# Cross-attention: GpSimd instead of SyncE issues the four transfers a pair that restack K's low part

## The reference

```
x = x + xattn(layernorm(x), ctx)     # 16 heads of 16, softmax over 256 keys, no mask and no scale
x = x + attn(layernorm(x))           # 16 heads of 64, causal
x = x + ffn(layernorm(x))            # 256 -> 1024 -> 256, gelu, fake-quantized weights and activations

xattn:  q = queries @ Wq;  k = keys @ Wk;  v = values @ Wv
        out = softmax(q k^T) v, heads joined, @ Wo
```

## Time and profile before

| | |
|---|---|
| runs | 670.81, 672.53 and 673.95 us; median 672.53 us |
| profiled execution | span 669.4 us from its first to its last instruction (the profile gives no other time of it) |
| PE busy | 608.3 us (91%) |
| DVE, ACT, POOL busy | 469.9, 388.8 and 197.3 us |
| PE clock granted | 0.987 of full on average |
| DMA | 58.44 MB, of which q1 moved 36.85, q0 12.20 and q10 8.78 |

### The profile page before, as it was taken

One profiled execution on the slowest core, in us unless ns is written; L12 is line 12 of the kernel. 1 busy time (PEld: TensorE's weight loads), 2 busy tenths in 40 slices (PEclk: granted clock), 3 DMA queues, 4 the chain that ended last, 5 costly groups with the idle time before them and its releaser, 6 DMA issues. The chain is left out here.

```text
span 669.4 us, 18523 instructions
## 1 busy us (share of the span) xinstructions
PE 608.3 (91%) x6772; PEld 520.5 (78%) x6796; DVE 469.9 (70%) x989; ACT 388.8 (58%) x1017; POOL 197.3 (29%) x308
## 2 busy tenths in 40 slices
PE   6788799999999899979998999999999999788997
PEld 3577788888989788865887898888888897644597
DVE  4376867878787677875789847575756656467797
ACT  3386767888888687874351515242424333357895
POOL 4736234545454544400020303030312111250000
PEclk9899989999999899999999999999999999899999
DMA  7888958585857586720300000000000000000012
GB/s 252 184 236 215 269 143 208 139 211 139 210 136 186 117 199 146 171 52 3 125 2 1 2 1 0 0 0 0 0 0 0 2 1 2 9 3 0 1 43 84
DMA packets 35597, 58.44 MB, mean 87 GB/s; under 512 B 6912, under 2 KB 15232, under 8 KB 35552
## 3 DMA queue, kind: packets, MB, share of 16 engines
q1 hardware_dynamic: 25008, 36.85, 21.8%
q0 software_dynamic: 5952, 12.20, 7.5%
q10 hardware_dynamic: 4592, 8.78, 4.8%
HBM read 17.96 MB, written 2.10 MB: 30 GB/s over the span
## 5 line engine op out<-in xcount | busy, mean ns | idle before, releaser
L573 ACT ACTIVATE Pr<-pS,nmax 128x256 f32<-128x256 f32 x256 | 119.8, 480 | 25.1 <-DVE nmax L677 24.5
L677 DVE TENSOR_REDUCE nmax<-pS 128x2 f32<-128x512 f32 x128 | 87.4, 683 | 35.6 <-PE pS L416 35.2
L899 POOL TENSOR_TENSOR a_Pr<-a_Pr,a_rinv 128x512 f32<-128x512 f32 x32 | 32.8, 1045 | 185.8 <-DVE a_rinv L1188 185.8
L426 PE MATMUL pT<-ident,Pr 128*128 128x128 f32 x512 | 78.5, 276 | 0.1
L416 PE MATMUL pS<-Kst,Qst 96*128 96x256 f32 x256 | 57.2, 305 | 21.6 <-DMA Kst<-KSl 16.6
L341 POOL TENSOR_TENSOR CSl<-CT,CSh 128x1024 fp32r<-128x1024 f32 x15 | 35.3, 2355 | 114.5 <-ACT CSh L566 114.5
L271 POOL DMA_DIRECT2D Qst<-QSh x124 | 62.0, 503 | 13.7 <-DVE QSl L649 6.9
L416 PEld LDWEIGHTS pS<-Kst,Qst 96*128 96x128 f32 x256 | 41.5, 192 | 30.2 <-issue 15.2
L1068 ACT ACTIVATE a_Pr<-a_Pr 128x512 f32<-128x512 f32 x32 | 20.2, 631 | 76.0 <-DVE a_Pr L1180 76.0
L426 PEld LDWEIGHTS pT<-ident,Pr 128*128 128x128 f32 x512 | 60.1, 142 | 0.8 <-ACT Pr L573 0.4
L573 ACT ACTIVATION_READ_ACCUMULATOR Pr<-pS,nmax 128x1 f32 x256 | 54.1, 211 | 0.0
(11 more groups left out here) (269 smaller groups left out, 1925.1 us busy)
## 6 DMA issues: line engine op xcount, KB each, us to landing
Kst<-KSh SPq DMA_DIRECT2D x126, 128.0 KB, 2.9
CT<-ctxT ACTq DMA_DIRECT2D x16, 512.0 KB, 5.6
Kst<-KSl SPq DMA_DIRECT2D x63, 128.0 KB, 3.7
Qst<-QSh POOLq DMA_DIRECT2D x124, 64.0 KB, 2.1
Qst<-QSl POOLq DMA_DIRECT2D x62, 64.0 KB, 2.1
X<-x SPq DMA_DIRECT2D x4, 512.0 KB, 9.0
out<-X SPq DMA_DIRECT2D x8, 256.0 KB, 2.2
raw<-awq SPq DMA_DIRECT2D x1, 1024.0 KB, 5.9
```

The source lines that it names most:

```text
L426: last = pe.transpose(pT[s % 2][:, t, k, :], Pr[s % 2][:, t, P * k:P * k + P], ident[:, :])
L573: act.activation(Pr[c % 2][:, t, :], pS[c % 2][:, t, :], ACT.Exp, bias=nmax[c % 2][:, t:t + 1], accum_out=rsum[par][:, c // 4, 2 * (c % 4) ...
L677: dve.tensor_reduce(nmax[s % 2][:, :], pS[s % 2][:, :, :], AX.X, ALU.max, negate=True).then_inc(maxed, 1)
L899: pool.tensor_tensor(rows, rows, rinv[s][:, :].unsqueeze(2).to_broadcast([P, 8, SQ]), ALU.mult).then_inc(weighted, 1)
```

## The change

SP now issues only the eight transfers of K's high part for the pairs 2 to 15 (`pieces=(0, 1)`). POOL issues the four of the low part (`pieces=(2,)`) behind its Q transfers of the same parity, after waits on the same two semaphores. The low part counts on semaphores of its own, `kst_low`, so PE, ACT and DVE wait for both counts. The prologue (pairs 0 and 1) keeps all twelve on SP and ACT, on `kst_in`.

```diff
     RESTACK = 12 * 16
+    LOW = 4 * 16
...
+        def k_restacked(eng, b, n):
+
+            eng.wait_ge(kst_in[b], RESTACK + (n - 1) * (RESTACK - LOW))
+            after(eng, kst_low[b], (n - 1) * LOW)
+
-        def restack_k(eng, b, r, chunks_done, groups=range(4)):
+        def restack_k(eng, b, r, chunks_done, groups=range(4), pieces=(0, 1, 2), done=None):
             after(eng, lo, r + 1)
             apart(eng, waited)
             after(eng, scores, chunks_done)
+            apart(eng, waited)
             for jj in groups:
-                for u, part in enumerate((HI, HI, LO)):
+                for u in pieces:
+                    part = (HI, HI, LO)[u]
                     eng.dma_start(f32(Kst[b][32 * u:32 * u + 32, jj:HP:4, :]),
-                                  f32(KS[part][32 * jj:32 * jj + 32, :, :])).then_inc(kst_in[b], 16)
+                                  f32(KS[part][32 * jj:32 * jj + 32, :, :])
+                                  ).then_inc((done or kst_in)[b], 16)
...
-                    restack_k(sp, 0, EV0 + EV * i + 5, CHUNKS * (p + 1))
+                    restack_k(sp, 0, EV0 + EV * i + 5, CHUNKS * (p + 1), pieces=(0, 1))
...
-                    restack_k(sp, 1, EV0 + EV * i + 9, CHUNKS * (p + 2))
+                    restack_k(sp, 1, EV0 + EV * i + 9, CHUNKS * (p + 2), pieces=(0, 1))
...
                     restack_q(pool, qst_in[0], 0, EV0 + EV * i + 3, CHUNKS * (2 * i + 1))
+                    restack_k(pool, 0, EV0 + EV * i + 5, CHUNKS * (2 * i + 1), pieces=(2,), done=kst_low)
                     ctx_low(1, 2 * i + 4)
                     restack_q(pool, qst_in[1], 1, EV0 + EV * i + 3, CHUNKS * (2 * i + 2))
+                    restack_k(pool, 1, EV0 + EV * i + 9, CHUNKS * (2 * i + 2), pieces=(2,), done=kst_low)
...
-                    pe.wait_ge(kst_in[par], RESTACK * (i + 1 + s // 16))
+                    k_restacked(pe, par, i + 1 + s // 16)
...
-                eng.wait_ge(kst_in[(ahead - 1) % 2], RESTACK * (i + (ahead + 1) // 2))
+                k_restacked(eng, (ahead - 1) % 2, i + (ahead + 1) // 2)
```

More of the change, by code:

```diff
@@ L219, in cross_attention @@
         kst_in = [sem(f"kst_in{i}") for i in range(2)]
+        kst_low = [sem(f"kst_low{i}") for i in range(2)]
         qst_sync, qst_in = sem("qst_sync"), [sem(f"qst_in{i}") for i in range(2)]
```

## The result

| | before | change |
|---|---|---|
| median of the runs | 672.23 us (20 runs) | 668.13 us (20 runs) |
| ratio | | 0.9948, 95% interval 0.9929 to 0.9966 |
| span of the profiled execution | 669.4 us | 666.3 us |

A forecast was written before the change was run, and what follows sets the result against it. PE, busy 91% and in order, was taken as the bound: its work plus its waits, chiefly for K. Terms 1.7 + 2.6 + 2.7 + 4.2 = 11.2 us off 672.5 gave 661.3 us, range 654 to 670.

The forecast's parts named there:

- POOL's price and cover: POOL's low-part issues: 0.7 us each (bounds 0.5 and 1.0), costing nothing, covered by POOL's 4.6 us idle stretch before CSl.
- Pair 11, 4.2 us: Pair 11's K: POOL's stop moves to pair 8, the wait falls from 2.96 to about 0.4, the clock holds: 4.2 us.
- Pairs 4 and 15, 1.7 us: PE's waits for K of 0.42 and 1.29 us both go, as SP is done 2.7 us sooner: 1.7 us gained.
- Pairs 5, 7, 9 and 13, 2.7 us: Odd pairs' K: two queues fill the engines better, 0.7 us a pair, giving back 2.7 of 3.62 us of waits.
- the reading of "0.88 busy" as SP's pace: Even pairs' K: with DMA engines 0.88 busy at 206 GB/s, SP's issuing was taken as the limit.
- the one with the engines as the bound: Rival: odd pairs' K and pair 3's land as before; gain 6.8 us, 665.7, or 3.3 us, 669.2; chance 0.20.
- the one in which the wait is only renamed: Rival: PE waits for K's high part instead, or ACT and DVE hold it up; 672.5 us; chance 0.10.
- Pairs 2 and 3, 2.6 us: Pair 2's wait of 1.61 us goes and pair 3's falls by 1.0 to 3.8: 2.6 us (bounds 1.6 and 8.9).
- The added waits, nothing: PE, ACT and DVE wait for a second count fourteen times; costed at nothing unless the low part is later.
- Short waits at their full length, windows of 32.42 us: Even pair to even pair: a wait costs its full length, so windows without pair 7's or 9's wait are 32.42 us.

The follow-up runs named there:

- e1: The kernel before, K still all on SP, with 13 small POOL transfers added in the prologue to move POOL's stop: 668.8 us, ratio 0.9926.
- e13: The change with PE waiting for K last, its high part after the low part: 667.5 us, ratio 0.9936.
- e14: e10 with PE waiting for K last: 666.3 us, ratio 0.9894 to the kernel before.
- e2: The change without POOL's transfers of K's low part from pair 2 on: 661.1 us, ratio 0.9792 to the kernel before.
- e3: The change with POOL issuing the low part in the order of head groups 2, 3, 0, 1: 665.1 us, ratio 0.9877 to the kernel before.
- e8: The change run again unaltered, with a second profile: 667.9 us, ratio 0.9912 to the kernel before.
- e9: e1 with three weight loads of quad 0 moved to the last quad, behind pair 15's K: 662.7 us, ratio 0.9847 to the kernel before.
- e17: e12 with PE waiting for K last, all of K on SP: 660.3 us, ratio 0.9830 to the kernel before.
- e18: e15 with ACT's second context load of each quad at step 7 instead of 2: 653.8 us, ratio 0.9741 to the kernel before.
- e5: e1 with SP holding quad 0's weight loads until pair 1's and pair 3's K have landed: 670.5 us, ratio 0.9964 to the kernel before.
- e12: e9 with ACT's second context load of each quad at step 7 instead of 2: 658.7 us, ratio 0.9787 to the kernel before.
- e16: e9 with K's low part, still from SP, counted on a semaphore of its own: 664.2 us, ratio 0.9880 to the kernel before.
- e7: e6 with POOL's low part in the order of head groups 2, 3, 0, 1: 667.8 us, ratio 0.9940 to the kernel before.
- e11: e10 with POOL's low part in the order of head groups 2, 3, 0, 1: 659.5 us, ratio 0.9809 to the kernel before.
- e15: e11 with PE waiting for K last: 658.8 us, ratio 0.9796 to the kernel before.
- e6: The change with SP holding quad 0's weight loads until pair 1's and pair 3's K have landed: 672.0 us, ratio 0.9987 to the kernel before.
- e10: The change with three weight loads of quad 0 moved to the last quad, behind pair 15's K: 667.9 us, ratio 0.9919 to the kernel before.

## Why the prediction was wrong, point by point

- **POOL's price and cover: right.** 0.54 us an issue (0.5 to 1.0, taken 0.7), and the CSl behind still waits for ACT, 3.09 us. POOL's timeline at pair 6, and at the stop:

```profile
131.39 2.14 POOL L289 DMA_DIRECT2D Kst<-KSl  x4 [0.33 <-issue]
136.62 2.36 POOL L351 TENSOR_TENSOR CSl<-CT,CSh 128x1024 fp32r<-128x1024 f32 x1 [3.09 <-ACT CSh L578]
...
165.11 1.09 POOL L289 DMA_DIRECT2D Kst<-KSl  x2
168.54 1.06 POOL L289 DMA_DIRECT2D Kst<-KSl  x2 [2.33 <-issue]
```

- **Pair 11, 4.2 us: right in its mechanism, 3.1 in size.** It still waits 1.30, where 0.4 were left by the forecast. The stop stands behind the 128th transfer, the second of pair 8's low part, as counted. That the pair doesn't wait long is worth the clock as well: 36.97 to 33.88. e1 shows that this term needs only the stop to move, not K.
- **Pairs 4 and 15, 1.7 us: right here.** Both waits are gone; pair 14 to 15 is 1.4 us shorter. That pair 15's goes is not certain, as e13 and e14 show.
- **Pairs 5, 7, 9 and 13, 2.7 us: failed, -1.0.** The step was "two queues fill the engines better", half of the difference between 238 and 352 GB/s. K lands at 9.65 and 11.93 us against 9.63 and 11.79: no sooner in odd pairs and, against the reading of "0.88 busy" as SP's pace, no sooner in even ones either. Amid pair 6's K the engines are 0.87 busy now and were 0.88; they move 232 GB/s and not 206 there, but K is not done the sooner. SP's blocks don't end after 5.2 us: only pair 3's does, and pair 15's nearly (5.57).

```profile
55.52 6.88 SPq L289 DMA_DIRECT2D Kst<-KSh  x8
...
70.05 5.11 SPq L289 DMA_DIRECT2D Kst<-KSh  x8
```

  A single issue of K on SP took up to 2.24 us (1.26 before), and a transfer that took 2.9 (high) and 3.7 us (low) to land takes 4.2 and 4.4. Two rivals came true in part. K lands as before whoever issues it, as in the one with the engines as the bound; e2 shows that fewer transfers do what the issuer doesn't. And PE waits for the high part with nearly the same sum, 14.9 of 16.6 us, as in the one in which the wait is only renamed. By the Trainium skill, DMA: Bandwidth & Descriptors, Issuing engines are not separate DMA queues, all issuers' transfers run on the same 16 engines and another issuer saves only the time of issuing; the landing times agree. That the engines are full is not shown: amid pair 6's K they are 0.87 busy, and in e3 the same bytes land 0.7 us sooner in another order.
- **Pairs 2 and 3, 2.6 us: failed, 0.** In the profiled execution of the change the waits are 0.27 and 6.67, but there the clock was at 0.66 behind pair 1's wait of 2.08 us, and PE came later to pair 2. In the change's second profile (e8) this didn't happen:

```profile
64.99 0.50 PE L428 MATMUL pS<-Kst,Qst 96*128 96x256 f32 x2 [1.27 <-DMA Kst<-KSh]
85.46 0.79 PE L428 MATMUL pS<-Kst,Qst 96*128 96x256 f32 x2 [5.11 <-DMA Kst<-KSh]
```

  1.27 + 5.11 is 6.38, and before it was 1.61 + 4.77, 6.38 too. What pair 2 gave back, pair 3 took, since the 2 MB of weights lie ahead of its high part as before. e9 shows what was to be had here: without them, the window from pair 2 to pair 4 is 33.66 us instead of 40.19.

```profile
66.32:99.98 33.66, 31.74 (x333) 28.52 (x333) 26.85 (x57) 27.73 (x89) 16.14 (x27) 1.00 0.68 168
```

- **The added waits, nothing: failed, by up to 1.0 us.** They add 0.2 us in each of five pairs; what that costs in time is not clear of the noise. "They hold nobody unless the low part is the later one" looked at which count is met last and not at the order in which they are taken: they stand behind the one that is.
- **Short waits at their full length, windows of 32.42 us: failed.** Windows without a wait are 33.07 (e2), 32.96 (e17) and 33.23 us (e18). Subtracting a wait from a window gives no floor: where the wait goes, PE is longer busy with the same matmuls (31.92 us in e2, 31.59 in the earlier trace rows). By the shares that e2 gave back in the four windows, the 2.7 us would have been some 0.9 even if the waits had gone as forecast (an estimate).

The measured time lies in the range because the rivals were in it. The rival of the engines gave 665.7, 2.4 us too little: pair 2's 1.6, which it had booked too, did not come, and the three windows from pair 4 to pair 10 are 1.7 us longer, for which no part of the prediction had a term. Part of that is K landing later in pair 5 (12.27 us behind SP's first issue, 11.43 before) and the added wait; the rest is open.

## What to carry to other kernels

A transfer that lands late is to be told apart by bytes before it is given to another issuer: drop some of it and see, and look at what else lies in its queues. When a count is split in two, wait last for the one that is met last, and look at what now stands behind the landing. A change that shifts an engine's list can gain by something that it never aimed at (here a stop that moved off a pair without slack): move that alone, and see what is left.

## What the runs showed that was not expected

- POOL stopped for 2.1 to 2.6 us, with no releaser, after its 128th transfer in every kernel without the 13 small ones; in the six with them (e1, e5, e9, e12, e16 and e17) it was 0.71 us after the 128th and 2.4 after the 159th. What it counts stays open.
- POOL's order of groups alone brought the even pairs' K 0.5 to 0.7 us sooner (e3, e7, e11, e15), and it made the kernel 0.5 to 1.1% faster in the three comparisons within a set with intervals apart: e7 against e6, e11 against e10, e15 against e14. In the old order both queues begin with the same 32 partitions of the source, in the new one with others; that this is the cause was argued, not shown.
- A wait of PE of 1.69 us was followed by a granted clock of 0.50 (e17, pair 15), and one of 2.59 in e8, at pair 1, by none: the clock was 1.00 over the next 5 us.
